# Local attention stage: projections and values by split four-byte parts, with a new order table

## The reference

```python
def attn_layer(x, Wqkv, qs, ksc, Wo):          # 16 heads of 64, window 64
    qkv = x @ Wqkv                             # 256 -> 3 * 1024
    q, k, v = jnp.split(qkv, 3, -1)            # then split into heads
    q = l2norm(q) * qs
    k = l2norm(k) * ksc
    q = q * cos * scale + rotate_half(q) * sin * scale
    k = k * cos * inv + rotate_half(k) * sin * inv
    out = local_attention(q, k, v)             # this window and the one before
    return out @ Wo
def ffn_layer(x, g, bln, W1, b1, W2, b2):
    hg = (layernorm(x) * g + bln) @ W1 + b1
    a, gate = jnp.split(hg, 2, -1)
    return a * gelu(gate) @ W2 + b2
```

## Time and profile before

| | |
|---|---|
| median of 3 runs | 4675.74 us (4674.79 to 4682.47) |
| profiled execution, its own time | 4666.11 us |
| its span, first to last instruction | 4664.2 us |
| Local stage in it, about | 1330 to 3117 us |
| mean granted TensorE clock | 0.962 of full |
| busy share of the span | PE 89%, DVE 67%, ACT 60%, POOL 39% |

### The profile page before, as it was taken

How to read it: one execution, slowest core, us unless ns; L and a number is a source line. 1 busy time by engine, 2 the same in 40 slices (tenths; PEclk the granted TensorE clock), 3 DMA queues, 4 the chain that set the end, 5 groups by cost and what they waited for, 6 DMA issues and landing times. The chain is left out here.

```text
span 4664.2 us, 82126 instructions
## 1 busy us (share of the span) xinstructions
PE 4155.7 (89%) x30120; PEld 2811.1 (60%) x30120; DVE 3116.0 (67%) x7290; ACT 2798.4 (60%) x5661; POOL 1805.0 (39%) x1876
## 2 busy tenths in 40 slices
PE   5899999988969999999999999957999999974895
PEld 3555555545736777777777777744555555543784
DVE  5677777767757666666666666535777777757655
ACT  2666666666837676676676676723666666652421
POOL 2322222204546555455455555413322222201843
PEclk8999999999989999999999999978999999996998
DMA  6655555525020001010010101016655555512255
GB/s 145 131 109 98 110 105 110 96 42 203 1 77 24 17 27 44 7 55 17 29 42 17 45 17 37 5 49 138 123 105 107 105 108 103 99 23 67 83 162 186
DMA packets 207469, 357.45 MB, mean 77 GB/s; under 512 B 26504, under 2 KB 116747, under 8 KB 203480
## 3 DMA queue, kind: packets, MB, share of 16 engines
q1 hardware_dynamic: 199488, 341.82, 32.4%
q0 software_dynamic: 7584, 10.39, 0.6%
HBM read 257.48 MB, written 114.98 MB: 80 GB/s over the span
## 5 line engine op out<-in xcount | busy, mean ns | idle before, releaser
L707 DVE TENSOR_REDUCE xa_m_part<-xa_ring 128x1 f32<-128x512 f32 x2048 | 1319.3, 686 | 497.6 <-PE xa_ring L856 482.6
L633 ACT ACTIVATE xa_ex<-xa_sc 128x1024 f32<-128x1024 f32 x1024 | 991.6, 1022 | 114.3 <-PE xa_sc L844 98.8
L856 PE MATMUL xa_ring<-xa_ks,xa_q_base 48*128 48x512 f32 x2048 | 519.5, 498 | 181.1 <-DVE xa_m_part L707 132.0
L1036 ACT ACTIVATE lt_p<-lt_bank,lt_stat,lt_rq 128x128 f32<-128x128 f32 (+1 forms) x768 | 365.0, 479 | 344.8 <-DVE lt_stat L1006 338.9
L1023 POOL TENSOR_SCALAR lt_p<-lt_p,lt_stat 128x192 f32<-128x192 f32 x384 | 345.8, 901 | 542.9 <-DVE lt_stat L1013 540.2
L870 PE MATMUL xa_pv<-xa_ex,xa_vs 128*17 128x256 f32 x8192 | 548.8, 386 | 0.0
L856 PEld LDWEIGHTS xa_ring<-xa_ks,xa_q_base 48*128 48x128 f32 x2048 | 201.5, 185 | 512.4 <-DVE xa_m_part L707 433.7
L844 PE MATMUL xa_sc<-xa_q_base,xa_ks 50*128 50x256 f32 x4096 | 423.3, 302 | 24.5 <-ACT xa_k L605 4.4
L844 PEld LDWEIGHTS xa_sc<-xa_q_base,xa_ks 50*128 50x128 f32 x4096 | 347.1, 187 | 115.2 <-ACT xa_vs L620 24.6
L1768 PE MATMUL lt_bank<-lt_wqk,lt_xt 128*128 128x512 f32 x768 | 365.6, 599 | 2.0 <-ACT lt_xt L1562 1.1
L555 POOL CAST xa_kp<-xa_k 128x512 fp32r<-128x512 f32 (+1 forms) x144 | 84.4, 586 | 655.7 <-ACT xa_k L613 314.9
(11 more groups left out here) (305 smaller groups left out, 8386.7 us busy)
## 6 DMA issues: line engine op xcount, KB each, us to landing
xa_ks<-keys SPq DMA_DIRECT2D x384, 256.0 KB, 9.3
keys<-xa_kp SPq DMA_DIRECT2D x128, 512.0 KB, 3.8
xa_cx<-in_ctx_t SPq DMA_DIRECT2D x64, 512.0 KB, 4.8
lt_wqk<-in_lt_wqkv SPq DMA_DIRECT2D x6, 2048.0 KB, 9.5
places<-in_moe_blank SPq DMA_DIRECT2D x47, 258.0 KB, 9.7
moe_xs<-places SPq DMA_DIRECT2D x47, 258.0 KB, 3.2
lt_w<-in_lt_w SPq DMA_DIRECT2D x6, 1536.0 KB, 7.5
xa_q_base<-xa_m_rows SPq DMA_DIRECT2D x512, 2.0 KB
```

The costliest lines, as they stand in the source:

```text
L633: act.activation(x.ex[:, n % x.NE, :, :], x.sc[n % 2][:, :, :], ACT.Exp).then_inc(*x.ex_done.one())
L707: dve.tensor_reduce(x.m_part[:, i % 2, qt, h, ch:ch + 1], x.bank(n + odd), AX.X, ALU.max).then_inc(*x.dve_out.one())
L856: pe.matmul(x.bank(n + odd), x.q_base[rows, pair, b * S + qt * P:b * S + (qt + 1) * P], x.ks[unit % x.NU][rows, pair % 4, ch * 512:(ch + 1 ...
L1036: act.activation(self.p[:, n % 5, to], s[:, at], ACT.Exp, bias=t3[:, 1, q:q + 1], scale=st.scale_of(b, h, slice(q, q + 1)) if st.scale is ...
```

## The change

- `proj` and `values` are done by parts (`by_parts`): six `float32r` matmuls of 512 columns in place of two float32 ones. `xt` gets a second part (`x_low`: DVE subtracts the high part from the PSUM bank, and only then is the bank free). The weights `wp` hold high and low parts of q, k and values, with one buffer.
- Each layer's weights are loaded in six pieces (`load_part`: q, k, values x two halves, two DMAs each) to `raw`, which lies in the FFN's buffers `u` and `gl` while these are idle, and split once a layer (`split`: two ACT copies, two DVE subtractions a piece). The gate steps wait for all splits so far.
- `v`, `tab`, `scl` and `b2` get one buffer in place of two. Values come later in a job (first half at ticks 18.66 and 23.95, second at 34.36 and 40.16).
- At the begin ACT copies `x` to `ot` (`stowed`), DVE normalises each batch behind its copy, and the park DMAs run from `ot` later. The first shift, the loads and the mask come in a new order, and PE waits for the mask only ahead of its first head.
- At the end the parked stream is fetched to `r_qk` at tick 30 of the last job, and three of the four batches are added, with their statistics, among the last job's steps (`fetched`).
- `TABLE`, `LOADS` and the tick constants are new.

```diff
+            self.wp = sb("wp", [P, 2, 3, KC, INNER], F32R)
+    FIRST = (-4.72, -0.15, 6.78, 8.89)
+    LOADS = ((11.93, "load_part", 3, (0, 0)), (9.24, "load_part", 3, (0, 1)), (16.46, "load_part", 3, (1, 0)),
+             (17.57, "load_part", 3, (1, 1)), (39.65, "load_part", 3, (2, 0)), (36.28, "load_part", 3, (2, 1)),
+             (7.51, "load_scl", 3, ()), (16.81, "tables", 3, ()), (80.75, "load_b2", 3, ()),
+             (15.94, "split", 3, (0, 0)), (17.09, "split", 3, (0, 1)), (20.2, "split", 3, (1, 0)),
+             (21.07, "split", 3, (1, 1)), (39.5, "split", 3, (2, 0)), (40.4, "split", 3, (2, 1)),
...
     def order(self):
-        put(("load_front", 0))
-        for b in range(2):
-            put(("shift", 0, b))
-        put(("load_mask",))
-        put(("load_values", 0))
-        put(("tables", 0))
+        put(("load_part", 0, 0, 0))
+        put(("shift", 0, 0))
+        put(("load_part", 0, 0, 1))
+        put(("load_scl", 0))
+        put(("load_small",))
+        put(("load_mask",))
+        put(("split", 0, 0, 0))
+        put(("features", 0, 0))
+        put(("x_low", 0, 0))
+        put(("tables", 0))
+        put(("split", 0, 0, 1))
+        for half in range(2):
+            put(("load_part", 0, 1, half))
+        put(("park",))
+        put(("shift", 0, 1))
...
+        timed.append((end + 30, len(timed), ("fetch",)))
+        for b in range(B):
+            timed.append((end + (56, 60, 64, 100)[b], len(timed), ("fetched", b)))
...
     def sp(self, sp):
+            if kind == "load_part":
+                on.wait_ge(*self.idle[step])
+                on.wait_ge(self.w_low, self.split[l, sec, half] - 2)
+                for k in range(KC):
+                    sp.dma_start(self.raw(half)[k], w[:, sec, k, at]).then_inc(*self.wp_in[sec][half].one())
...
     def act(self, act):
+            elif kind == "split":
+                on.wait_ge(self.wp_in[sec][half], KC * (l + 1))
+                if l:
+                    last = ("values", l - 1, B - 1, 1, half) if sec == 2 else ("proj", l - 1, B - 1, 1, sec, half)
+                    on.wait_ge(self.gen_full, self.use[last] + 1)
+                for k, raw in enumerate(self.raw(half)):
+                    act.activation(self.wp[:, 0, sec, k, half * 512:half * 512 + 512], raw,
+                                   ACT.Copy).then_inc(*self.w_high.one())
...
     def dve(self, dve):
+            elif kind == "split":
+                for k, raw in enumerate(self.raw(half)):
+                    on.wait_ge(self.w_high, KC * self.split[l, sec, half] - KC + k + 1)
+                    low = dve.tensor_tensor(self.wp[:, 1, sec, k, at], raw, self.wp[:, 0, sec, k, at].bitcast(F32),
+                                            ALU.subtract)
+                low.then_inc(*self.w_low.one())
+            elif kind == "fetched":
+                b, = a
+                on.wait_ge(self.park_in, 1)
+                on.wait_ge(self.fin, 2 * self.job(DEPTH - 1, b) + 2)
+                for t in (2 * b, 2 * b + 1):
+                    old = self.r_qk[:, t // 4, t % 4 * D:(t % 4 + 1) * D]
+                    dve.tensor_tensor(y[:, t, :], y[:, t, :], old, ALU.add).then_inc(*self.x_chain.one())
+                    on.wait_ge(self.x_chain, self.x_chain.n)
+                    tile_stats(c, dve, on, t, self.x_chain)
...
+    def by_parts(self, pe, bank, par, tile, sec, half):
+        m = 0
+        for k in range(KC):
+            for xpart, wpart in PARTS:
+                mm = pe.matmul(bank[:, :], self.xt[:, par, xpart, k, tile * P:(tile + 1) * P],
+                               self.wp[:, wpart, sec, k, half * 512:half * 512 + 512],
+                               start=(m == 0), stop=(m == 3 * KC - 1))
+                m += 1
+        return mm
     def pe(self, pe):
-        on.wait_ge(self.mask_ready, 1)
-        on.wait_ge(self.p_zero, 1)
             elif kind == "proj":
-                for k in range(KC):
-                    mm = pe.matmul(bank[:, :], self.xt[:, par, k, tile * P:(tile + 1) * P],
-                                   self.wqk[:, l % 2, k, col:col + 512], start=(k == 0), stop=(k == KC - 1))
-                mm.then_inc(*self.gen_full.one())
+                on.wait_ge(self.w_low, self.split[l, sec, half])
+                self.by_parts(pe, bank, par, tile, sec, half).then_inc(*self.gen_full.one())
```

More of the change, by code:

```diff
@@ L1314 @@
     scale = None
[L1315 to L1327, removed]
[4 rows of a table removed]
@@ L1377, in __init__ @@
         self.use = {s: n for n, s in enumerate(banked)}
+        for j in range(2, DEPTH * B):
+            assert self.use["features", *divmod(j, B)] > self.use["values", *divmod(j - 2, B), 1, 1]
+        self.split = {s[1:]: n + 1 for n, s in enumerate(s for s in self.plan if s[0] == "split")}
+        self.idle, self.splits = {}, {}
+        after, loads, splits = (self.gen_full, 0), 0, 0
+        for s in self.plan:
+            if s[0] == "load_part":
+                self.idle[s], loads = after, loads + 1
+            elif s[0] == "split":
+                splits += 1
+            elif s[0] == "gate":
+                assert loads == splits
+                self.splits[s], after = splits, None
+            elif s[0] == "w2" and s[3] == 1:
+                after = self.gen_full, self.use[s] + 1
     def job(self, l, b):
@@ L1474, in sp @@
                 l, = a
[L1475 to L1478 removed]
+                on.wait_ge(self.fin, 2 * B * l)
+                sp.dma_start(self.b2[:, :], g("lt_b2")[l]).then_inc(*self.b2_in.one())
             elif kind == "load_back":
@@ L1552, in act @@
     def act(self, act):
-        on = Waits(act)
+        c, on = self.c, Waits(act)
+        for b in range(B):
+            act.activation(self.stowed_of(b), c.x[:, 2 * b:2 * b + 2, :], ACT.Copy).then_inc(*self.stowed.one())
         for step in self.plan:
@@ L1595, in act @@
                 on.wait_ge(self.gen_full, self.use["w1", l, b, mc + 1] + 1)
+                on.wait_ge(self.w_low, self.splits[step])
                 for m in (mc, mc + 1):
@@ L1785, in pe @@
                 on.wait_ge(*self.freed(("features", l, b)))
-                on.wait_ge(self.wv_in, l + 1)
-                for k in range(KC):
-                    mm = pe.matmul(bank[:, :], self.xt[:, par, k, tile * P:(tile + 1) * P],
-                                   self.wval[:, k, half * 512:half * 512 + 512],
-                                   start=(k == 0), stop=(k == KC - 1))
-                mm.then_inc(*self.gen_full.one())
+                on.wait_ge(self.w_low, self.split[l, 2, half])
+                self.by_parts(pe, bank, par, tile, 2, half).then_inc(*self.gen_full.one())
             elif kind == "attend":
@@ L1800, in pe @@
                     on.wait_ge(self.rq_done, 2 * j + 2)
+                    on.wait_ge(self.mask_ready, 1)
+                    on.wait_ge(self.p_zero, 1)
                     on.wait_ge(self.zeros, 3)
-                if what == "apply" and n % H == 0:
+                if what == "apply" and n % (H // 2) == 0:
                     for tile in range(2):
-                        for half in range(2):
-                            on.wait_ge(*self.freed(("values", *divmod(j, B), tile, half)))
+                        on.wait_ge(*self.freed(("values", *divmod(j, B), tile, 2 * (n % H) // H)))
                 self.at.pe_step(pe, on, self, a[0])
```

139 lines of the change are left out of this document (84 added, 55 removed), and 8 rows, old and new, of the table TABLE.

## The result

| | before | after |
|---|---|---|
| median | 4675.26 us (4672.91 to 4682.47, 4 runs) | 4740.68 us (4728.96 to 4748.18, 4 runs) |
| after / before | | 1.0131, interval 1.0115 to 1.0148 |
| span of the profiled execution | 4664.2 us | 4741.7 us |
| Local, from L145 on POOL at its begin to the same line of the next stage | 1786.7 us | 1846.5 us |
| mean granted TensorE clock | 0.962 | 0.950 |

What follows compares the result with a forecast made beforehand. The prediction took PE to bound Local; -72 (matmuls), -8 (begin), -4.8 (end) and +8 (edges) sum to -76.8, so the median was forecast at 4675.7 - 76.8 = 4598.9 us, range 4564 to 4650.

Steps and rivals of the forecast that it cites:

- the last paragraph of part 2: SP's queue in Local: a load behind a shift's one-row DMA still comes 2 ticks before its split, costing nothing.
- The slower one: Layer edges: weight pieces pass one at a time through two raw halves, unhidden 201 us over five edges, 4792; chance 0.08.
- Part 1: Projection and value matmuls in Local: 288 steps fall from 1.72 to 1.47 us, saving 72 us, from 43 to 101.
- The rival without a price for the change of kind: Matmul steps: the first weight load hides under float32 work, a step costs 1.37, 29 us more gain, 4570; chance 0.18.
- an estimate of 0.75: Matmul steps: three passes in place of four would give 1.29 us a step, 124 us saved; the prediction's rows spoke against it.
- Part 2, the edges: Splits at layer edges: DVE over by 1 us, PE stalls 1.6 us a layer, 8 us over five, bounds 0 and 28.
- The three heads: Attention: three heads, 4.5 ticks or 12.7 us between a head's scores and its transposes, soak up some us of delay.
- DVE's chain: Layer edges: the 72 subtractions are held by POOL operations where DVE is over-subscribed, 30 us in all, 4629; chance 0.22.
- its price by holds: DVE's subtractions: a mean hold of 0.42 us each if they meet POOL at random, 30 us in all.
- Part 3, the begin: Local's begin: first projection at 1349.5, 9.4 us earlier; net gain 8 us, from 2 to 11.
- Part 4, the end: Local's end: two tiles, not eight, behind the last `w2`, -6.0, third batch's tiles +1.2; net -4.8, from -6 to -2.
- those named for "right": Local: 1728 records, pitch near 0.245, PE over 97% busy in mid-Local, first projection near 1349.5, two tiles behind last `w2`.

Runs made afterwards that it cites:

- e1: The changed kernel with the next layer's shift due at tick 79.0 in place of 85.67, so ahead of `fs` in SP's queue: 4660.21 us, 0.9968 of before.
- e2: e1 with two float32 matmuls in place of six on parts, loads and splits kept: 4716.0 us, 1.0086 of before.
- e9: e7 again, timed in rounds: 4644.66 us, 0.9943 of before, Local 1752.0 us.
- e3: e1 without the weight loads and splits of layers 1 to 5, all using layer 0's parts: 4607.15 us, 0.9861 of before.
- e6: e1 with the two splits of k behind the scaling of k (ticks 21.3 and 21.4): 4655.22 us in one run, Local 1765.8.
- e12: e7 with the low parts of k in layers 1 to 5 subtracted by POOL, not DVE: 4658.76 us, 0.9968 of before.
- e4: The kernel before with its shift due at tick 79.0 in place of 82.7, so ahead of `fs`: 4716.92 us, 1.0092 of before.
- e5: e1 with POOL's two zeroings held until DVE has normalised all of x: 4650.98 us in one run, Local 1751.9.
- e7: e5 with the mask's load also moved ahead of the first shift: 4638.28 us in one run, Local 1752.1.

## Why the prediction was wrong

**The step that failed** is the last paragraph of part 2: "SP has the six loads of a layer among its shifts ... a load behind it still comes 2 ticks ahead of its split. Nothing." It looked at what stands behind a shift, never at what stands ahead of it. `SHIFT` had moved from 82.7 to 85.67, `fs` from 56.72 to 59.01, and `w2` tile 1 from 83.33 to 78.38. Read as one queue: the shift's data came 5 ticks earlier, its issue 3 ticks later, behind an `fs` that itself stood 2.3 ticks later, with data 1.4 ticks later (`wo` tile 1 moved from 56.3 to 57.72). The prediction knew the length of the one-row DMA. Two of them in a row are 10.5 us, `features` stood 2.79 ticks or 7.9 us after `shift` in the table; that sum was to be had from the diff and the earlier trace rows, and it was not made. Where the prediction has "Nothing", e1 measures 87.6 us of Local: 74 are the waits that go, and PE's busy time falls by 30 with the clock back, while other waits grow by some 17.

No rival had this mechanism. The slower one (pieces serial through two raw halves) did not happen: PE waited for `w_low` once in the stage, for 2.0 us. It named the sign and not the cause.

**Part 1 was right.** Step 1.47 forecast, 1.47 measured; 72 us forecast, 68.6 by e2, and 2.96 a plain job by e9. The rival without a price for the change of kind (1.37 a step) is out. The Trainium skill (FP8 and Floating Point Precision, "TensorE Precision Notes") has four passes for true float32, from which the prediction worked out an estimate of 0.75 for three in their place. The steps of this case do not bear it out: 1.47 / 1.72 is 0.85.

**Part 2, the edges, was mis-sized**: 1.6 us each forecast, bound 5.6, measured 7.5 by e3 and 6.7 by the job times of e9. The sum that found DVE over by 1 us in 14.7 was right in kind (15.17 of 16 busy). What it left out: a PE step waits for one place in DVE's queue, not for the mean, and a subtraction is held now and then (0.76 on the mean). Moving the work (e6) or handing part of it to POOL (e12) only changed which wait showed it; that the three banks taken in turn pass the delay on would fit this, but no run shows it by itself. The three heads that were to soak up a delay cover attention, but the steps that stood were the transposes of q and k. The rival "DVE's chain" named the right engine and put the time at 4629; the versions without the queue's fault stand at 4645 to 4660. Of its price by holds, 0.42 us an operation, little was there: 0.76 on the mean against 0.68 for the undisturbed form.

**The plain jobs carry small waits too**: e3, without any edges, still has 8.6 us for `ft` (L1920), where before has none to speak of. They were in no term. The new order is a likely cause, but no run shows it: e2 has the same order with float32 steps and 4.2 us, e4 the old table and 10.5.

**Part 3, the begin**: forecast 9.4 us earlier and 8 net. The first projection came 5.8 earlier (24.3 against 30.1 us into the stage), and of that nothing was left: PE idled 13.6 us more in the first 240. Two causes were not in the sum: the zeroings beside the normalised tiles, 7.0 us by e5, and PE's waits for the scaled k in the first 200 us, 15.7 us in after against 4.6 in before, of which the splits of k ahead of the first scaling are 1.7 (e7). With both changes of e7 the first projection stands at 16.0, 14.1 earlier than before, and Local is still only 34.5 shorter than before, while the matmuls alone give 68.6.

**Part 4, the end, was right in what it looked at**: from the last `w2` addition to the end of the stage's work it takes 3.0 us against 8.8, so -5.8 where -6.0 was forecast. From the last `wo` addition, which takes in the third batch's two tiles, it is 39.4 us against 45.4, so -6.0 where the net was put at -4.8, from -6 to -2. The `w2` step that no longer fills the wait for `fs`, 3.2 us, was in no term.

**The sum.** Forecast -76.8, measured +59.8, a miss of 136.6: the queue 87.6, the edges 37.4 - 8 = 29.4, and 19.6 for the rest. e3, which has neither the queue's fault nor the edges, shows where the rest lies: against before, PE's idle time is 11.5 us more in the first 240 us of Local, 10.3 more in the middle and 2.2 less in the last 220, 19.6 in all. That is the begin and the small waits of the plain jobs.

**The signs.** Of those named for "right", the records, their pitch and the two tiles behind the last `w2` came true; the first projection did not, nor did PE's share of the middle (93.5%, where over 97 was asked). Of those for the rival "DVE's chain", PE did idle at each edge and the subtractions' records were longer than 0.61, but what released PE was the scaled k behind them. The others did not come. A wait in each job at `features` was not on the list.

## What to carry to other kernels

When a change re-times the steps of a kernel with one DMA queue, write out that queue for one period, with each entry's length, when its data are ready and who stands ahead of it. In both kernels here a step that waited there made all behind it wait, and one number in a table moved Local by 88 us (e1) and by 48 (e4). An engine that is some 65% busy on the mean can be the bound of a 16 us stretch: put work that comes once a period into the period's own sum, next to the steps that stand behind it in the same queue. And read the first of several equal periods apart from the rest: in e9 the plain job showed the forecast gain (2.96 us for 3.0), while the whole of Local gained 35 of a forecast 77.

## What the runs showed of the hardware

- **A DMA of one partition's row holds its queue for long.** In after the part of `fs` with one row took 4.4 to 4.8 us of SP's queue, that of `shift` 4.6 to 6.3 and once 12.0, against 0.7 (once 2.1) for those with 127 or 128 rows, though they move the least. The median for `shift` was 5.9, right behind the one of `fs`, and 4.7 in before, where the queue paused between the two.
- **Some DVE and POOL operations exclude each other, and the later one waits.** At the begin DVE's first two tiles were held until the first and the second zeroing were over: 8.86 us for 2.67 us of work. The Trainium skill (SBUF — State Buffer, "SBUF: two separate sides") says that the port pair which the two share is locked for the whole instruction by whichever comes first, for a DVE operation in a 2-port mode against any GpSimd one; the trace agrees on the wait, with an operation on one SBUF tensor against a memset, but no row tells in which mode it ran. In the edge of e9 both directions show, here between operations with two SBUF inputs each: POOL's addition of 1.27 us took 1.62 as it came 0.2 us after a subtraction had begun, and DVE's next subtraction ended only 0.6 us behind the addition, so that three took 2.98 for 1.9.
- **Short gaps cost clock.** Waits of 2.8 to 4.7 us, one a job, put the granted clock at 0.97 over the middle where it was 1.00 in before and e1, and with them PE's busy time over the stage was 30 us more than in e1. Not each gap did it: 15 of 20.
